# Cross-attention value weighing for two key-value heads at a time in 512-column matmuls, with ten expert-weight buffers and fourteen token buffers, in a decoder layer on one core

## What is computed

```python
# cross-attention, with H = 32, KV = 8, G = 4 query heads per key-value head, D = 16
scores = jnp.einsum('bkgsd,bktd->bkgst', qh, kh) / scale
weights = jax.nn.softmax(scores, axis=-1)
out = jnp.einsum('bkgst,bktd->bkgsd', weights, vh)
# experts: E = 32, CAP = 128 slots each, H = 512, F = 256
h = jax.nn.silu(jnp.einsum('ech,ehf->ecf', buf, w1)) * jnp.einsum('ech,ehf->ecf', buf, w3)
ob = jnp.einsum('ecf,efh->ech', h, w2)
# x = x + self_attn(ln(x)); x = x + cross_attn(ln(x), ctx, ctx); x = x + ffn(ln(x))
```

## Time and profile before

| what | value |
|---|---|
| median of the runs | 1013.92 us |
| profiled execution | 1013.2 us, span 1011.0 us |
| TensorE, weight loads | 916.0 us (91%), 556.4 us (55%) |
| VectorE | 569.5 us (56%) |
| ScalarE | 346.9 us (34%) |
| GpSimd | 325.7 us (32%) |
| HBM read, written | 70.90 MB, 16.88 MB |

### The profile page before, as it was taken

How to read it: one execution, slowest core, us unless ns; L and a number is a source line. 1 busy time by engine, 2 the same in 40 slices (tenths; PEclk the granted TensorE clock), 3 DMA queues, 4 the chain that set the end, 5 groups by cost and what they waited for, 6 DMA issues and landing times.

```text
span 1011.0 us, 16294 instructions
## 1 busy us (share of the span) xinstructions
PE 916.0 (91%) x6192; PEld 556.4 (55%) x6192; DVE 569.5 (56%) x1286; ACT 346.9 (34%) x699; POOL 325.7 (32%) x320
## 2 busy tenths in 40 slices
PE   5778999999999999999999999799999899999980
PEld 4435546645754764764774674364677444444440
DVE  1455747876786785795786687684342222222220
ACT  4121065165256246326417425427200122222210
POOL 4010002110520540341251153042324255546774
PEclk9988599799999999999999999989999999999995
DMA  4455003302301400520330330280513699999643
GB/s 142 124 217 127 21 3 87 82 4 68 100 24 38 125 9 2 151 61 2 103 87 24 77 92 3 63 292 2 185 66 95 220 314 346 332 323 309 136 66 32
DMA packets 101920, 115.14 MB, mean 114 GB/s; under 512 B 12482, under 2 KB 80352, under 8 KB 101840
## 3 DMA queue, kind: packets, MB, share of 16 engines
q1 hardware_dynamic: 83908, 94.42, 30.3%
q0 software_dynamic: 14480, 16.55, 8.4%
q10 hardware_dynamic: 3456, 3.15, 1.2%
HBM read 70.90 MB, written 16.88 MB: 87 GB/s over the span
## 4 chain that ended last, share of the span: by engine, by line
PE 57%; DVE 17%; DMA 12%; issue 6%; ACT 5%; POOL 2%; ACTq 0%; POOLq 0%; DVEq 0%
DMA out<-arena,half_ids 7%; PE qa L1497 6%; DVE mxx L1029 5%; PE qa L1291 4%; PE pt L1209 4%; PE qx L1435 4%; PE vb L1446 4%; PE qx L1377 4%; PE qa L1209 4%; DMA out<-res,half_ids 3%; ACT arena L638 3%; PE qa L1631 3%; DVE mx L997 2%; PE qa L1325 2%; POOL out L625 2%
## 5 line engine op out<-in xcount | busy, mean ns | idle before, releaser
L1029 DVE TENSOR_REDUCE mxx<-qx 128x2 f32<-128x512 f32 x256 | 168.6, 686 | 47.0 <-PE qx L1377 45.7
L638 ACT ACTIVATE arena<-qx 128x512 f32<-128x512 f32 x256 | 146.4, 602 | 127.5 <-PE qx L1435 111.8
L492 POOL TENSOR_TENSOR rstd<-mv,power 128x2 f32<-128x2 f32 x24 | 17.2, 717 | 363.2 <-DVE mv L865 363.2
L638 ACT ACTIVATE arena<-qa 128x512 f32<-128x512 f32 (+2 forms) x125 | 67.2, 540 | 187.4 <-PE qa L1631 98.5
L1377 PE MATMUL qx<-arena 96*128 96x256 bf16 x512 | 104.5, 294 | 13.6 <-DVE mxx L1029 9.6
L1631 PE MATMUL qa<-arena 128*128 128x512 f32 x256 | 115.2, 593 | 1.1 <-ACT arena L638 1.1
L1435 PE MATMUL qx<-arena 98*128 98x512 bf16 x256 | 94.6, 391 | 6.9 <-ACT arena L638 2.9
L625 POOL DMA_INDIRECT out<-arena,half_ids x44 | 68.5, 1558 | 56.0 <-DMA out<-arena,half_ids 28.4
L1446 PE MATMUL vb<-arena 128*32 128x256 f32 x1024 | 82.2, 393 | 1.6 <-ACT arena L638 0.4
L1377 PEld LDWEIGHTS qx<-arena 96*128 96x128 bf16 x512 | 47.1, 103 | 58.0 <-DVE mxx L1029 26.3
L1162 DVE SCALAR_TENSOR_TENSOR arena<-arena,qa 128x256 f32<-128x256 f32 x32 | 13.5, 421 | 109.9 <-ACT arena L638 109.9
(11 more groups left out here) (205 smaller groups left out, 1583.5 us busy)
## 6 DMA issues: line engine op xcount, KB each, us to landing
arena<-in_L_ffn_w SPq DMA_DIRECT2D x96, 512.0 KB, 6.7
qs<-arena SPq DMA_DIRECT2D x24, 384.0 KB, 5.0
arena<-arena SPq DMA_DIRECT2D x72, 128.0 KB, 3.5
res<-in_x SPq DMA_DIRECT2D x8, 512.0 KB, 6.9
xnd<-arena SPq DMA_DIRECT2D x8, 512.0 KB, 5.9
ks<-arena SPq DMA_DIRECT2D x48, 64.0 KB, 1.9
arena<-arena SPq DMA_DIRECT2D x48, 64.0 KB
arena<-arena ACTq DMA_DIRECT2D x24, 128.0 KB, 3.6
```

What stands on the lines that cost most here:

```text
L638: nc.scalar.activation(dst, src, func, **kw).then_inc(s[signal], 1)
L1029: v_.reduce_max(mxx[:, col:col + 3:2], xbank[v % 2].rearrange("p (h n) -> p h n", h=2), AX.X).then_inc(s["x_max"], 1)
```

## The change

Four things are changed.

**Value weighing.** `xweigh` now does two key-value heads for one half of the context at once: 8 calls instead of 16, each four float32 matmuls of 512 columns. The units are put in another order, so that four units in a row belong to one call: it stands behind `xkeyed(v)` for v = 5, 9, ..., 29, and the last behind everything. The exponential gets six buffers instead of four; the score banks stay two. `pair_out` stands behind exponentials 11, 19 and 27 in place of 9, 17 and 25. `cross_out` undoes the other order with two VectorE products in place of one.

**Expert weights.** Ten places in place of nine. Three experts instead of four are loaded at the start of step 8, expert 6 while the shared part runs, experts 7 to 9 behind it. From expert 10 on w1 is asked for when the up projection of expert e-10 is done, w2 when a down projection is, w3 one result later.

**Tokens.** Fourteen places in place of eight; fetches 8 to 13 stand ahead of the first output. The space comes from letting the second and third norm share one buffer (`xn3 = xn2`), for which VectorE and ScalarE each get a wait on the other's last reader.

```diff
-EU = 9
-FETCH = 8
+EU = 10
+FETCH = 14
+EXRING = 6
...
-        xn3 = place(2 * D)
+        xn3 = xn2
...
-        ex = [place(512) for _ in range(4)]
+        ex = [place(512) for _ in range(EXRING)]
...
-        XW = XU // 2
+        XW = XU // 4
...
# SyncE
-                    for e in range(4):
+                    for e in range(3):
                         expert_in(e)
...
-            for e in range(4, 7):
+            for e in range(3, 6):
                 expert_in(e)
             for b in range(POOLED // 6, B):
+                if b == B - 2:
+                    sp.wait_ge(s["t3_t"], B * 2)
+                    sp.wait_ge(s["xnd_out"], B * 16)
+                    expert_in(6)
                 sp.wait_ge(s["sh_added"], b * 2 + 2)
                 sp.dma_start(out_rows[:, b * 2:b * 2 + 2], tokens(b)).then_inc(final_out[b], 16)
             for e in range(7, EU):
                 expert_in(e)
-            for e in range(EU, NE):
-                sp.wait_ge(s["down_done"], e - EU + 1)
-                expert_in(e)
+            for e in range(EU, NE + 1):
+                if e < NE:
+                    sp.wait_ge(s["up_done"], e - EU + 1)
+                    gate_or_up_in(e, 0)
+                if e > EU:
+                    sp.wait_ge(s["down_done"], e - EU)
+                    down_in(e - 1)
+                    sp.wait_ge(s["y_ready"], e - EU)
+                if e < NE:
+                    gate_or_up_in(e, 1)
...
# GpSimd, behind the wait for the eight outputs of the shared part
+            for e in range(8, FETCH):
+                fetch(e)
...
# ScalarE
+                    act.wait_ge(s["n_t"], min(k, B))
                     norm_apply(3, k - 2, xn3)
...
-                    if v >= 4:
-                        act.wait_ge(s["xpv_done"], k * XW - XW + (v - 4) // 2 + 1)
-                    copy(ex[v % 4], xbank[v % 2], "xe_ready", ACT.Exp, scale=float(XD) ** -0.5)
-                    if v % 8 == 1 and v > 8:
+                    if v >= EXRING:
+                        act.wait_ge(s["xpv_done"], k * XW - XW + (v - EXRING) // 4 + 1)
+                    copy(ex[v % EXRING], xbank[v % 2], "xe_ready", ACT.Exp, scale=float(XD) ** -0.5)
+                    if v % 8 == 3 and v > 8:
                         pair_out(v // 8 - 1)
...
# VectorE
+                    if g:
+                        dve.wait_ge(s["t3_t"], 2 * k - 2)
+                        dve.wait_ge(s["xnd_out"], k * 16 - 16)
                     norm_apply(2, k, xn2)
...
# TensorE
-                    kv, t = w // 2, w % 2
-                    pe.wait_ge(s["xe_ready"], k * XU - XU + 2 * w + 2)
+                    pair, t = w // 2, w % 2
+                    pe.wait_ge(s["xe_ready"], k * XU - XU + 4 * w + 4)
...
-                        op = mm(vb[at_:at_ + 32, kv % 2 * S:kv % 2 * S + S], vx[:, t, kv, :],
-                                ex[(2 * w + g4 // 2) % 4][:, g4 % 2 * S:g4 % 2 * S + S], start=t == 0, stop=t == 1,
-                                tile_position=(0, at_))
+                        op = mm(vb[at_:at_ + 32, :], vx[:, t, pair * 2 + g4 // 2, :], ex[(4 * w + g4) % EXRING],
+                                start=t == 0, stop=t == 1, tile_position=(0, at_))
...
                     xkeyed(v)
-                    if v >= 3 and v % 2 == 1:
-                        xweigh((v - 3) // 2)
+                    if v >= 5 and v % 4 == 1:
+                        xweigh((v - 5) // 4)
```

More of the change, by code:

```diff
@@ L247, in build @@
         fetched = ([view(arena, fetch_at + r * D, D) for r in range(3)]
-                   + [view(res, (2 * 2 + r) * D, D) for r in range(4)] + [view(arena, ht_at + 4 * P, D)])
-        assert len(fetched) == FETCH and len(ye) == YR and 4 * D <= xr_at - ox_at and fetch_at + 3 * D <= xn3_at
+                   + [view(res, (2 * 2 + r) * D, D) for r in range(4)] + [view(arena, ht_at + 4 * P, D)]
+                   + [view(res, (2 * slot_ + t) * D, D) for slot_ in (5, 0, 1) for t in range(2)])
+        assert len(fetched) == FETCH and len(ye) == YR and 4 * D <= xr_at - ox_at and fetch_at + 3 * D <= ox_at
         iw = sb("iw", [P, NE * 2], U32)
@@ L371, in tokens, with gate_or_up_in, down_in @@
                 return tile(b, 0, 2).rearrange("p (t d) -> p t d", t=2)
+            def gate_or_up_in(e, a):
+                sp.dma_start(h13[e % EU][:, a], (w1, w3)[a][e].rearrange("(c p) f -> p c f", c=DC)
+                             ).then_inc(wg_in[e % EU], 16)
+            def down_in(e):
+                sp.dma_start(h2[e % EU], w2[e].rearrange("(c p) d -> p c d", c=2)).then_inc(wg_in[e % EU], 16)
             def expert_in(e):
[L374 to L377 removed]
+                for a in range(2):
+                    gate_or_up_in(e, a)
+                down_in(e)
             go(tokens(0), rows[:, 0:2], "x_in")
@@ L1429, in xkeyed @@
                 def xkeyed(v):
-                    kv, t, half = v // 4, v // 2 % 2, v % 2
+                    kv, t, half = v // 8 * 2 + v // 2 % 2, v // 4 % 2, v % 2
                     if v >= 2:
```

34 lines of the change are left out of this document (18 added, 16 removed).

## The result

The changed kernel takes **1029.49 us** (median of 4 runs, 1026.92 to 1029.77), the one before, run beside it, 1015.87 (4 runs, 1013.15 to 1019.25): a ratio of 1.0137, 95% interval 1.0098 to 1.0176. That is 13.6 us slower. The prediction said 1021, within 1005 to 1030, which is 7.1 us more than the 1013.9 it started from. The sign holds and the range holds by 0.5 us. The loss is nearly twice the one forecast: the value is 8.5 us short, of which 2 us are the slower runs of the kernel before beside it, and the time lies above the band of 1016 to 1027 that got a chance of 0.50.

The account below looks back on a forecast made before the run. Bound: the score, exponential and bank-release round through two banks, with the experts' output chain setting the end. Sum: 1011.0 + 11.4 (cross-attention) - 4 (experts) = 1018.4 of span, giving 1021 us; range 1005 to 1030.

Parts of the forecast that it names:

- What bounds the kernel: Cross-attention's second pass: not simply 82 us of TensorE time; score, exponential and bank release through two banks set the pace.
- The weighing's own price: Value weighing on TensorE: 512 columns take 1.00 us against 0.57; work per four units falls from 2.20 to 1.98.
- Rival A: Whole kernel: TensorE is the bound and the 14 us saving is kept, 996 us; chance 0.12.
- The chain of four units: Second pass, two score banks: four units take 2.88 us instead of 2.45, 0.43 more, as ScalarE starves.
- Step 8: Step 8's second pass, the pure case with nothing to hide the loss: 3.6 us longer.
- Steps 1 to 6: Cross-attention in the middle steps: net 1.3 us longer per step, 7.8 in six.
- Rival C: Cross-attention: work between units gives ScalarE its time back, cross part even, experts -4, 1010 us; chance 0.18.
- The experts: Expert weights and outputs: weights end earlier, outputs 7.7 us apart while weights flow, then 4.42; 4 us less.
- rival D: Experts: the change doesn't do there what it says, as outputs set their own pace, 1025 us; chance 0.10.
- Rival B: Experts: outputs starve at 8.9 us each, 6 us more there, 1031 us in all; chance 0.10.
- The queues: Expert weight loads: by the skill's rule a longer queue would not delay outputs, 7.28 us each, 4 us less.
- The small parts: Extra `cross_out` product and the two waits for the shared norm buffer: both 0; without cover, 1 us.

Follow-up runs that it names:

- short: The changed kernel with each weighing from step 2 on streaming only 256 of its 512 columns; 1025.77 us, step 8's second pass 26.01 us.
- banks8: The changed kernel with four score banks, eight exponential buffers and weighings two units later in step 8; 1027.95 us, step 8's second pass 23.21 us.
- cross_only: The changed kernel with nine weight places, eight token places and the old loop of weight loads, new weighing kept; 1035.0 us, ratio 1.0158 to before.
- experts_only: The changed kernel with the old 256-column weighing, unit order and four exponential buffers, everything else new; 1020.03 us, ratio 0.9992 to before.
- burst: The changed kernel with an expert's three weight loads asked for at once, ten weight and fourteen token places kept; 1032.21 us, ratio 1.0115 to before.
- fetch8: The changed kernel with eight token places instead of fourteen; 1029.29 us, ratio 1.0074 to before.
- halves8: The changed kernel with each step 8 weighing cut into two 256-column calls, two units apart, and eight exponential buffers; 1023.62 us, step 8's second pass 26.14 us.
- before_banks: The kernel before with four score banks, six exponential buffers and weighings two units later in step 8; 1019.23 us, ratio 0.997 to before.
- again: The changed kernel run once more without edit, on another chip; 1029.44 us.
- banks_old: experts_only with four score banks, six exponential buffers and weighings two units later in step 8; 1012.91 us, ratio 0.9967 to before.

## Why the prediction was right or wrong, point by point

- **What bounds the kernel: right.** That the weighing was no simple TensorE time but part of a round with ScalarE through two banks is shown by short (half the columns, 2.45 per four units all the same) and by banks8 (the same columns, two banks more, 1.97).
- **The weighing's own price: right.** 1.00 us was said, 1.00 measured. TensorE's work per four units, 2.20 old and 1.98 new, came out as 2.21 and 1.97 where four banks let it show. Rival A needed TensorE to be the bound; it isn't, and its 996 us is far off.
- **The chain of four units: right**, 2.88 said, 2.89 measured, with ScalarE idle for 0.66 to 0.72.
- **Step 8: right**, +3.6 said, +3.67 measured.
- **Steps 1 to 6: right.** From the second projection to the counting matmul 16.06 was worked out, 15.95 measured; per step +1.3, in six +7.8, measured +8.5 (1.3 to 1.5 a step). Between the two projections it was -0.65, said -0.66; ahead of the first it was some +0.5 a step where +0.3 was said. Rival C, that the other work in a step fills the gaps, falls with it. The Trainium skill, TensorEngine Tiling (Array Packing), PSUM Bottleneck, says that tiling doesn't speed up the evacuation, here the exponentials. Short (2.45) and banks8 (1.97) agree.
- **The experts: wrong in size.** The term was -4 (its own sum gives 994.7 for expert 31 and so -4.3, not the 995.0 written) and is 0 (-0.15) in the pair of profiles, which is rival D's case. Its parts: 7.7 us per output was said and 7.68 measured, and the last weights were asked for exactly when worked out, 924.5 + 16. The outputs' faster pace was put at a landing of these weights 5.5 us later. But a load took longer from issue to landing, 10.4 us in the median (page above) against 6.7 on the page of before; the eight loads of w2 asked for from 901 to 940.5 took 9.0 to 12.0. So the last landed between 949.5 and 952.5 and not at 946, and the slow pace held up to expert 17. Against the sum that is (950.65 - 820.17) - (16.3 x 7.7 + 0.7 x 4.42) = +1.9, then 5.12 - 4.42 = +0.7, and from there on 4.55 per output instead of 4.42, +1.7: together 4.3. This is what the pair shows; against cross_only on its chip, experts_only's outputs are 4.1 us shorter, while its timed ratio to before is worth -0.8 (-3.3 to +1.6); by that interval a gain of up to 3.3 us is possible, and the 4 of the prediction just not. The prediction had given the earlier end of the weights its gain in full and charged the same bytes in less time only in the pace, not in the landing and not in the tail. Rival B's mechanism (8.9 us per output) didn't occur, though its 1031 us lies nearest.
- **The queues.** The Trainium skill, DMA: Bandwidth & Descriptors, Queues, rings and completion order, says that a DMA engine takes its queues in turn, packet by packet. From this the prediction worked out that a longer queue would not slow an output, which would have been 7.28 us per output. The kernels with ten places show 7.54 to 7.68, those with nine 7.30 to 7.55: in this kernel more weights asked for at once do mostly go with slower outputs. Whether the queue or the memory causes it was not separated.
- **The start: not foreseen.** The prediction was made against one profiled execution of before that had the shorter start (143.4). The changed kernel's two profiles had the longer one (148.0). These 4.5 us are half of the 9.1 by which the spans' difference, 16.5, exceeds the predicted 7.4; the experts are 3.9 more; the rest, 0.7, are the steps and the end. A profile of before with the longer start would have been nearer, so a part of the miss is chance, and so is that the range still held, by 0.5 us.
- **The small parts: right.** From step 7 into step 8 it is -0.4, and experts_only, which has the shared norm buffer and its waits, takes as long as before.

## What to carry to other kernels

Before merging small matmuls into a long one, look at who is fed between them: with n banks the feeding engine may be away no longer than the consumer takes for n pieces, here an estimate of 2 x 0.53 us less the 0.43 to start again, that is 0.63. A block of 0.57 us stayed under it and one of 1.00 us broke it; no length between was run. The merge pays once the banks cover it (1.97 us per four units against 2.89). And where a load is brought forward, charge the transfers beside it, in their pace, in the landing of the load itself and in the tail.

## What the runs showed of the hardware

**The start falls in one of two ways, by where the clock is halved.** At about 28 us TensorE runs the four matmuls of `keep_busy(4)`, eight records, whose result nothing reads, and then waits. The profile says "issue", but in the code it is the wait for the self-attention's operands, which SyncE loads (`ks_in`, `qs_in`). Before:

```profile
27.62 5.29 PE L1192 MATMUL qx<-arena,ident 128*128 128x512 f32 x8
34.41 0.38 PE L1323 MATMUL qa<-masks,identb 128*128 128x512 bf16 x1 [1.50 <-issue]
```

and after:

```profile
27.96 3.60 PE L1223 MATMUL qx<-arena,ident 128*128 128x512 f32 x8
34.70 0.58 PE L1354 MATMUL qa<-masks,identb 128*128 128x512 bf16 x1 [3.14 <-issue]
```

Before, the granted clock was 0.51 from 28 to 30 us and 0.64 from 30 to 32, and 1.00 from 32 on: the half speed (1.2 of 2.4 GHz) fell on the matmuls that nobody reads, which took 5.29 us in place of 3.60, and the wait behind them shrank by about as much, from 3.14 to 1.50. After, the clock was 1.00 up to 33 us, fell while TensorE stood waiting (0.84 from 33 to 34), and stayed at 0.50 to beyond 48: here it fell on the self-attention's scores, and the same matmul takes 0.58 instead of 0.38. The wait ends between 34.1 and 35.1 in all thirteen profiles, so its length follows from the clock and not the other way round. In five (before, cross_only, burst, fetch8, halves8) the `keep_busy` matmuls take 5.2 to 5.3 us, the wait 1.5, and the projection of step 1 is reached at 141.4 to 145.5. In the other eight they take 3.6, the wait 3.1 to 3.2, and it is reached at 147.5 to 149.9. What decides where the clock falls is open. Over a whole execution the time goes with the clock, and by much beside such a change: 17 runs of the kernel before on one chip took 1009.8 to 1021.9 us, with mean granted clocks of 0.952 to 0.962; the seven at 0.960 and above took 1009.8 to 1013.1 us, the ten at 0.957 and below 1016.0 to 1021.9.

**Some chips add a stall in every step.** In the profile of before_banks, on another chip, four more waits of TensorE put down to issue stand before the line of that first score matmul (L1330 there), and five in the self-attention's weighing (us in total, times, longest):

```profile
PE qa L1330 <- issue: 4.1, 5, 3.2
PE va L1501 <- issue: 1.5, 5, 0.3
```

Its steps take 82.1 to 83.0 us, where before, of the same code there and also at full clock, takes 81.2 to 81.5 (82.0 the first). In the three steps between before's counting matmuls at 407.09 and 651.09, compared row by row, the two are equal up to the self-attention's first weighings, some 50 us in, and behind them before_banks is 0.8 to 1.5 us later. The profiles of before, after, again and banks_old have no such waits, those of the other nine, on three chips, all have the four more before that line (again and banks_old are from a fourth), so it seems to go with the chip; the cause is open. It is a reason to compare the second passes, which repeat to 0.02 us, and not whole steps, across chips.

**Longer pieces didn't help the weights.** Pieces of 4 KB instead of 1 and 2 KB left the outputs' stretch at 199.0 us, within the 194.9 to 199.2 of the other kernels with nine places.
